# Feed-forward columns computed for sorted tokens, in a fused attention and column layer

## The reference

```python
# attention: 16 heads of 16 numbers
q, k, v = heads(xn @ Wq + bq), heads(xn @ Wk + bk), heads(xn @ Wv + bv)
q = q * cos + rotate_half(q) * sin
k = k * cos + rotate_half(k) * sin
att = (einsum('bhid,bhjd->bhij', q, k) + rel_bias_table[bucket]) / sqrt(16)
att = softmax(where(causal, att, -inf))
attention = merge(einsum('bhij,bhjd->bhid', att, v)) @ Wp + bp
...
# feed-forward: 16 columns of 64 neurons, one column chosen for each token
similarity = einsum('bsd,cd->bsc', l2norm(xn), l2norm(col_emb))
gates = sigmoid(gelu(xn @ gate_w1 + gate_b1) @ gate_w2 + gate_b2)
logits = similarity + gates
_, top_idx = top_k(logits, 1)
weights = one_hot(top_idx) * softmax(logits)
cols = gelu(einsum('bsd,cdn->bscn', xn, W_cols) + b_cols) * weights[..., None]
y = cols.reshape(B, S, 1024) @ proj_w + proj_b + xn
ffn = layernorm(y) * ln_g + ln_b
```

## Time and profile before

| | |
|---|---|
| median of 3 runs | 2119.39 us (2117.95 to 2120.36) |
| profiled execution | 2120.78 us |
| its span | 2118.7 us, 41887 instructions |
| PE busy | 1881.9 us, 89% |
| DVE busy | 1602.9 us, 76% |
| ACT busy | 1101.7 us, 52% |
| POOL busy | 632.2 us, 30% |
| mean granted TensorE clock | 0.962 |
| DMA | 144.77 MB, 199400 packets |

### The profile page before, as it was taken

One profiled execution on the slowest core, in us unless ns is written; L12 is line 12 of the kernel. 1 busy time (PEld: TensorE's weight loads), 2 busy tenths in 40 slices (PEclk: granted clock), 3 DMA queues, 4 the chain that ended last, 5 costly groups with the idle time before them and its releaser, 6 DMA issues.

```text
span 2118.7 us, 41887 instructions
## 1 busy us (share of the span) xinstructions
PE 1881.9 (89%) x11110; PEld 1051.4 (50%) x11110; DVE 1602.9 (76%) x5859; ACT 1101.7 (52%) x2142; POOL 632.2 (30%) x848
## 2 busy tenths in 40 slices
PE   4887899999999999999999999999999999997677
PEld 2654455555445555555455554455555554443223
DVE  2335788888888688878888778887888788887773
ACT  2231555555565555556555455565555555644444
POOL 5463333223333322233333123333332233300000
PEclk9988899999999999999999999999999999998887
DMA  8422212232222122232212222221222322112101
GB/s 221 130 60 76 59 50 65 56 84 81 66 60 72 49 68 64 60 93 68 59 47 69 70 75 66 65 76 47 70 56 64 86 81 60 47 52 58 45 14 41
DMA packets 199400, 144.77 MB, mean 68 GB/s; under 512 B 60427, under 2 KB 186779, under 8 KB 199148
## 3 DMA queue, kind: packets, MB, share of 16 engines
q1 hardware_dynamic: 199148, 141.85, 24.2%
HBM read 90.59 MB, written 56.69 MB: 70 GB/s over the span
## 4 chain that ended last, share of the span: by engine, by line
PE 58%; DVE 21%; issue 11%; POOL 3%; SPq 3%; ACT 3%; DMA 1%; DVEq 0%; ACTq 0%; POOLq 0%
PE scores L1081 10%; PE bank L1092 9%; PE o_bank L1000 8%; PE scores L983 7%; PE bank L1038 5%; DVE scores L1153 5%; PE rows L1020 4%; DVE rows L1178 4%; PE rows L1026 3%; DVE maxima L1174 3%; PE rows L1024 2%; PE scores L1083 2%; PE bank L1110 2%; DVE maxima L1183 2%; ACT probs L869 2%
## 5 line engine op out<-in xcount | busy, mean ns | idle before, releaser
L869 ACT ACTIVATE probs<-scores 128x512 f32<-128x512 f32 (+1 forms) x1280 | 670.7, 555 | 522.5 <-DVE scores L1153 238.4
L983 PE MATMUL scores<-stack_q,stack_k 99*128 99x512 bf16 (+3 forms) x1536 | 439.0, 337 | 85.2 <-ACT probs L869 60.4
L1178 DVE CUSTOM_DVE_ANT_0 rows<-rows,near_rows 128x256 f32<-128x256 f32 (+1 forms) x1024 | 416.1, 409 | 28.3 <-PE rows L1020 24.6
L1153 DVE TENSOR_TENSOR scores<-scores,near_cols 128x256 f32<-128x256 f32 x768 | 333.6, 443 | 84.5 <-PE scores L983 84.0
L1174 DVE TENSOR_REDUCE maxima<-rows 128x1 f32<-128x256 f32 (+1 forms) x768 | 304.9, 397 | 121.4 <-PE rows L1024 119.3
L1000 PE MATMUL o_bank<-probs,v_aug 128*32 128x512 f32 (+3 forms) x3072 | 320.7, 505 | 3.2 <-ACT probs L869 3.2
L1020 PE MATMUL rows<-stack_k,stack_q 96*128 96x256 bf16 (+1 forms) x1024 | 276.2, 276 | 41.5 <-DVE maxima L1178 24.0
L1081 PE MATMUL scores<-xn_t,w_cols 128*128 128x256 f32 x1024 | 286.9, 404 | 2.5 <-ACT others_t L915 2.5
L1183 DVE TENSOR_REDUCE maxima<-rows 128x1 f32<-128x128 f32 (+3 forms) x512 | 248.9, 486 | 50.3 <-PE rows L1026 48.1
L1092 PE MATMUL bank<-w_proj,act_t 128*128 128x256 f32 x1024 | 270.4, 402 | 16.4 <-DVE y L1211 14.7
L983 PEld LDWEIGHTS scores<-stack_q,stack_k 99*128 99x128 bf16 x1536 | 142.3, 99 | 217.4 <-ACT probs L869 138.1
(11 more groups left out here) (109 smaller groups left out, 2270.2 us busy)
## 6 DMA issues: line engine op xcount, KB each, us to landing
parts_d<-part SPq DMA_DIRECT2D x96, 256.0 KB, 2.5
stack_q<-parts_d SPq DMA_DIRECT2D x384, 64.0 KB, 2.6
stack_k<-parts_d SPq DMA_DIRECT2D x384, 64.0 KB, 2.6
x<-in_x_dram SPq DMA_DIRECT2D x32, 256.0 KB, 3.5
v_d<-v SPq DMA_DIRECT2D x32, 256.0 KB, 2.5
rest_d<-rest SPq DMA_DIRECT2D x32, 256.0 KB, 2.7
v_in<-v_d SPq DMA_DIRECT2D x32, 256.0 KB, 3.3
result<-rest_d SPq DMA_DIRECT2D x32, 256.0 KB, 3.9
```

What stands on the lines that cost most here:

```text
L869: act.activation(probs[:, (g * NS + s) % PROBS, h, 0:width], ring[(rings + ring_n[1]) % RING][:, 0:width], ACT.Exp, scale=float(D) ** -0.5 ...
L983: ins = pe.matmul(ring[(rings + ring_n[1]) % RING][:, c0:c0 + w], stack_k[g % 2][:, h, kb * P:(kb + 1) * P], stack_q[g % 2][:, h, q0:q0 + ...
L1153: dve.tensor_tensor(tile[:, 0:2 * P], tile[:, 0:2 * P], near, ALU.add))
L1178: dve.tensor_tensor_reduce(tile[:, 0:w], tile[:, 0:w], near_rows[:, ag * GH + h, 2 * P - w:2 * P], 1.0, LOWEST, ALU.add, ALU.max, maxima[: ...
```

## The change

**Routing.** Each token's column is now used to sort the tokens of a batch. `center` writes xn into `xn_all`, a row of 258 numbers for each token of the batch, and `weigh` writes the weight of the choice behind it. `choose` keeps the one-hot choice in `chosen_one`. In group 2, when the last chunk of the next batch is through, `tally` sums the choices with eight small products and thirteen small DVE operations give the padded start of each column (a multiple of 64 rows) and, for each of 32 tiles of 64 rows, its column's index; `route` gives each token's row by eight more products and four DVE operations. POOL scatters the rows to `xs_d` by eight indirect transfers.

**The columns of sorted tokens.** A batch is 32 tiles (`SLOTS_B` = 2048 rows, padding included), done in four steps, one a group. SP loads a step's 512 rows and, for each of its eight tiles, reads the column's index from SBUF and loads this column's weights `w1` and `w2` from DRAM: 17 transfers (`ffn_in` in the opening of group 3, `ffn_next` after slot 29 of groups 0, 1 and 3). `xs_turn`, `neurons` and `columns` are computed in slots 13 to 24; ACT applies gelu and the weight, POOL adds xn, SP stores to `ys_d`. `gather` in group 2 (after slot 27) brings the rows back in the tokens' order by eight indirect transfers of POOL, before the scatter of the next batch.

**Finishing.** The second layer norm and the sum move from every group to groups 3 (chunks 0 and 1) and 0 (chunks 2 and 3): `finish_begun` after slots 2 and 12, `finish` after 7 and 16; `again` loads x once more into `result`, and `rest_d`, `rest` and `skip` are gone. `columns` pieces, `neurons` pieces, `mask_turn` and `pick` are gone from opening, slots 1 to 6 and closing. `x` of the next chunk is loaded after `x_turn`, not after `mask_turn`.

**The shift.** The three transfers into `stack_q` are issued by ACT, straight after its copy.

```diff
-BESIDE = {1: [('columns', 3)],
-          2: [('widen', None), ('columns', 4)],
...
+BESIDE = {2: [('widen', None), ('finish_begun', 0)],
+          4: [('center', None)],
+          6: [('x_turn', None)],
+          7: [('finish', 0)],
+          10: [('qk_begun', 0), ('qk', 0)],
+          12: [('load_q', None), ('v', 0), ('finish_begun', 1)],
+          13: [('xs_turn', 0)],
+          14: [('qk_begun', 1)],
+          15: [('qk', 1), ('xs_turn', 1)],
+          16: [('finish', 1)],
+          18: [('neurons', None), ('hidden', None)],
           19: [('v', 1)],
           21: [('gate', None), ('o_turn', 0)],
+          22: [('columns', 0)],
           23: [('qk_turn', 0), ('choose', None)],
+          24: [('columns', 1)],
           25: [('left', 0), ('tie', None), ('middle', 0)],
           26: [('choice', None), ('y_turn', 0)],
+          27: [('weigh', None), ('gather', None)],
           28: [('load_k', None), ('project_begun', 0)],
-          29: [('project', 0)],
-          30: [('qk_turn', 1)],
-          31: [('left', 1), ('mask_turn', None)],
-          32: [('y_turn', 1)],
+          29: [('project', 0), ('ffn_next', None)],
+          30: [('qk_turn', 1), ('tally', None)],
+          31: [('left', 1)],
+          32: [('y_turn', 1), ('route', None)],
           34: [('middle', 1)],
...
-OPENING = [("stats", None), ("columns", 0), ("columns", 1), ("columns", 2)]
+OPENING = [("again", 0), ("ffn_in", None), ("stats", None)]
-CLOSING = [("load", None), ("neurons", (0, 0)), ("neurons", (0, 1)), ("pv", NS - 1), ("o_out", 1),
-           ("neurons", (1, 0)), ("neurons", (1, 1)), ("neurons", (2, 0)), ("shift", None),
-           ("neurons", (2, 1)), ("neurons", (3, 0)), ("neurons", (3, 1)), ("o_turn", 1), ("shift_turn", None)]
+CLOSING = [("load", None), ("pv", NS - 1), ("o_out", 1), ("shift", None), ("o_turn", 1), ("shift_turn", None)]
...
+                    elif stage in ("ffn_in", "ffn_next"):
...
+                        wait(sp, ys_out, step * 16)
+                        sp.dma_start(xs[:, :, :], xs_d[k * HALVES * SLOT:(k + 1) * HALVES * SLOT, :]
+                                     .rearrange("(q p) f -> p q f", p=P)).then_inc(ffn_loaded, 16)
+                        for half in range(HALVES):
+                            at = k * HALVES + half
+                            col = sp.value_load(column_i[at:at + 1, 0:1], min_val=0, max_val=E - 1)
+                            sp.dma_start(w1[:, half, :, :], w1_d[col]).then_inc(ffn_loaded, 16)
+                            lane = (half % 2) * N
+                            sp.dma_start(w2[lane:lane + N, half // 2, :], w2_d[col]).then_inc(ffn_loaded, 16)
...
+                    elif stage == "route":
...
+                        for j in range(NT):
+                            pool.indirect_dma_start(xs_d[:, :], bass.IndirectOffsetOnAxis(slot_i[:, j:j + 1], 0),
+                                                    xn_all[:, j, :], None).then_inc(scattered[j >= CT], 16)
+                    elif stage == "gather":
...
+                        pool.wait_ge(ys_out, (b + 1) * (FFN_STEPS * 16))
...
+                            pool.indirect_dma_start(gathered_y[:, j, :], None, ys_d[:, :],
+                                                    bass.IndirectOffsetOnAxis(slot_kept[:, j:j + 1], 0)) \
+                                .then_inc(gathered, 16)
...
+                    elif stage == "finish_begun":
+                        pb, m = projected(b, g), finishing_of(b, g, arg)
+                        pool.wait_ge(gathered, pb * (NT * 16) + NT * 16)
+                        for t in range(CT):
+                            ins = pool.tensor_tensor(gathered_y[:, arg * CT + t, :], gathered_y[:, arg * CT + t, :],
+                                                     b_proj[:, :], ALU.add)
+                        ins.then_inc(y2_made, 1)
...
+                        act.wait_ge(bank_drained[i], use + 2)
+                        for r in range(3):
+                            act.dma_start(stack_q[ag % 2][STACK + r:STACK + r + 1].rearrange("r h (q t) -> r (h q) t", t=P),
+                                          shift_t[r * GH * NT:(r + 1) * GH * NT, :]).then_inc(shift_in, 16)
...
+                        for pair in range(PAIRS):
+                            for h in range(2):
+                                for k in range(KC):
+                                    ins = pe.matmul(tile[h * N:(h + 1) * N, pair * SLOT:(pair + 1) * SLOT],
+                                                    w1[:, pair * 2 + h, k, :],
+                                                    xs_t[:, pair, k, h * SLOT:(h + 1) * SLOT],
+                                                    start=(k == 0), stop=(k == KC - 1))
...
+                        for q in range(2):
+                            for h in range(2):
+                                lanes = slice(h * N, (h + 1) * N)
+                                ins = pe.matmul(bank[lanes, q * C:(q + 1) * C], act_t[lanes, 2 * arg + q, :],
+                                                w2[lanes, 2 * arg + q, 0:C], start=True, stop=True)
...
+                    elif stage == "finish_begun":
+                        m = finishing_of(b, g, arg)
+                        dve.wait_ge(y2_made, m + 1)
+                        for t in range(CT):
+                            ins = dve.bn_stats(stats2[:, t, :], gathered_y[:, arg * CT + t, :])
```

More of the change, by code:

```diff
@@ L164 @@
            "project": 9}
 DVE_TIME = {"score": 2, "center": 7, "qk": 6, "v": 5, "gate": 1, "choose": 3, "tie": 4, "choice": 3,
-            "y2_stats": 10, "mask_turn": 3, "left": 6, "o_turn": 6, "project": 6, "finish": 7, "stats": 10}
+            "weigh": 3, "left": 6, "o_turn": 6, "project": 6, "finish": 7, "stats": 10, "finish_begun": 9,
+            "columns": 8, "tally": 15, "route": 8}
 def with_rows(plan, first, last, rows):
@@ L211, in add @@
             needs = self.used["hidden"]
+        if stage == "columns":
+            needs = self.used["neurons"]
         if stage == "pv":
```

503 lines of the change are left out of this document (301 added, 202 removed).

## The result

| | before | after |
|---|---|---|
| median | 2118.67 us (2115.51 to 2120.36) | 2476.86 us (2465.64 to 2485.59) |
| ratio | | 1.169, 95% interval 1.164 to 1.174 |
| span of the profiled execution | 2118.7 us | 2475.3 us |
| mean granted clock | 0.962 | 0.819 |

The account below looks back on a forecast made before the run. DVE was taken to bound the slots, PE only the stretch between groups. Groups -78, new waits +108, prologue 0 and last batch -5 gave +25 us on the median 2119.4: 2145 us, range 2000 to 2240.

Parts of the forecast that it names:

- DVE as the limit: In the forty score slots DVE, 92% busy, sets the pace, also when PE is less loaded.
- the sign: The whole kernel becomes slower, by 25 us; chance of slower 0.54.
- the stop at slot 2: At finish_begun DVE waits for POOL's bias, behind widen and v_in: 3.3 us in group 0, 9 in group 3.
- third rival: A register read on SP costs a landing, 3.3 us; group 0 stops 22 us, 2320 us in all; chance 0.10.
- 58+9+1.4: Group 3: 58.0 us without new waits, 9 us stop at slot 2, 1.4 us at the second finish_begun.
- A group without new waits: Boundary, slots and clock allowance sum to 58.0 us, 2.9 less than 60.9; 27 groups give -78 us.
- DVE stays at 49.8 us a group: DVE's busy time a group: weighted adds go, tally and route come; it is a floor for the group.
- SP before group 0: SP finishes its loads and reads 17 us after load_k, before slot 39 at 21 us, so just on time.
- Group 3 and the indirect transfers: Sixteen indirect transfers in group 2, 1.0 us of POOL each, make v_in late; DVE stops 9 us in group 3.
- The sum of new waits: DVE's stops in groups 3 and 0 total 15 us a batch (5 to 35), +108 us over seven batches.
- The ends: Prologue: PE's relief and a new serial row cancel, zero (-30 to +20); the last batch's groups -5 us.
- the forecast's 0.50: Chance of the forecast case, waits of about 15 us a batch; its own range is 2080 to 2220 us.

Follow-up runs that it names:

- e4: The kernel before with most products of the columns left out and nothing added: 2072.8 us, ratio 0.979.
- e13: The changed kernel with 6 of the 24 short products of neurons and columns a group kept, so columns are not computed: 2437.6 us.
- e2: The changed kernel with a constant column index for each 64-row tile, so SP reads no index: 2414.5 us.
- e3: The changed kernel with POOL's sixteen indirect transfers a batch replaced by plain ones of the same bytes, tokens not sorted: 2400.0 us.
- e17: The changed kernel with POOL's sixteen transfers plain, no column index read by SP and no second layer norm: 2197.8 us.

## Why the prediction was wrong

The measured time lies above the range because three steps failed at once: the price of SP's set of loads with the reads in it, the indirect transfers as POOL's time only, and the gain of a group without new waits.

**Right:** DVE as the limit, so that PE's relief is worth little (e4); the sign; in group 0 the stop at slot 2 and its chain (SP, v_in, widen, POOL's sum, DVE); the third rival's direction (a read that costs more makes the stop of group 0 grow, and the loss is large), though a read holds the queue for 0.8 us and not for a landing of 3.3.

**Right by luck:** group 3, with 68.3 us for the 58+9+1.4 that it said. The stop of 9 us in it was 0.0 to 0.2; the time went elsewhere, into the slots.

**A group without new waits, 58.0 us (55.5 to 59.5):** groups 1 are 60.8 (58.9 before), so a gain of 2.9 us a group, 78 in all, was never there. The step took the boundary and the slots apart and gave each its best. The boundary did shrink: from the activation of slot 39 to that of the next slot 0 before took 12.5+5.8 = 18.3 us (around 1071.9) and after 5.0+5.4 = 10.4 (around 1236.1). But from slot 0 to 39 it went from 40.9 to 50.7 us; rows that had stood in the boundary stand in the slots now. The columns' products stand there too, but they are about 1 us of it: e13, without them, has 48.4 us from slot 0 to 39 of group 1 on the mean, after 49.5, before 40.8. That it is the rows, and how much the half clock of 14.6 us in this group adds, is argued and not shown. e4 puts the relief of PE at some 45 us, 21 of it in the prologue. "DVE stays at 49.8 us a group" failed as well: it is busy 51.8 us a group on the mean, before 49.4.

**SP before group 0, "just on time":** this step failed for group 0. 16 weight loads, the load of the rows and eight reads were priced at 0.4 us each, 10.0 us; the set takes 15.2. The issues were 0.34 to 0.55, close; the read was 0.8 instead of 0.4. The Trainium skill ("DMA: Bandwidth & Descriptors", "Latency and other measured facts") has about 0.6 us as the floor of a tensor_load, nearer than the row that the sum used. Two more things went the same way. What stands ahead of the set and behind it took 11.0 us for 6.9, so that load began 1095.80-1069.64 = 26.2 us behind load_k and not 17. And slot 39 came 17 us behind load_k and not 21, so load, which was to wait for slot 39, began 9 us behind it. v_in went out 18.6 us behind slot 39 where the sum had 8.6, and the stop of 3.3 us became 10.7. e2 gives 62 us back.

**Group 3 and the indirect transfers:** 1.0 us each was right in kind (1.25 us measured). What had no term at all is that DVE, PE and ACT nearly stand still in these 20 us: the step had counted the transfers as POOL's time only. e3 prices it at 77 us. It also undid the step's own conclusion. The last part came later than said (24.7 us behind load_k for 18.7), but so did slot 39 (30 us for 17), and v_in was there in time; with plain transfers DVE does stop there, for 5 us.

**The sum of new waits, 15 us a batch (5 to 35):** the batch grew by 47.9 us. The upper bound was set by raising one price at a time; e17 shows prices that add. Between 79 and 150 of the 358 us are in none of the three; 25 of them are in batch 0, and but for the 27 us of the two small operations their cause stays open.

**The ends:** zero and -5 were taken. The prologue took 5.5 us more, and the last batch's four groups lost 21 us instead of gaining 5.

Three small slips in its sums change nothing: seven batches of 15 us are 105 and not 108; 35.3 less 27 is 8 us and not 9; and a fifth of the forecast's 0.50 is 0.10, more than its chance of "faster" has room for.

## What to carry to other kernels

Price an addition first in the queue that issues it, each step of it with all that stands behind it in order, and only then on the engine that it relieves: here 219 us of PE's time were given up, and the index reads in SP's queue alone cost 62. When the bound is another engine, measure the gain of leaving the work out before building its replacement (e4: 2%). Look at what a moved stage waits for in its new place: leaving the second norm out gave 140 us, and only 71 of them were its own work. When a predicted time comes out right, look for the wait that was to make it: group 3 had the time and not the wait.

## What the runs showed of the hardware

Indirect transfers issued by POOL one behind the other slow the others: in 20.1 us with sixteen of them DVE was busy for 0.39 to 0.41 of the time, and PE's row products reached it up to 13 us late. Eight in a row did less (0.58, up to 6.3 us late), and plain transfers of the same bytes made none late (77 us of the kernel). A register read from SBUF on SP, with its check, puts about 0.8 us between two issues; leaving it out saved 0.7. Neither was expected in this size. Two small operations of DVE, 0.2 us each alone, took 0.4 to 1.1 us where they overlapped an operation of POOL. TensorE's clock stood at 0.50 for 15 to 36 us of each group in the changed kernel against 0 to 5 before; a filler took 7 to 10 us of that away in two groups, won 1.0 us in each and nothing in all, so what it costs isn't known.
